# Decoder kernel on one core: router logits of the expert layer by feature in column strips, and a slot search with rounded 32-bit tables

## What is computed

```
full_logits = x @ gate_w.T                      # T = 4096 tokens, 8 dynamic experts and 1 fixed
# sparse mixer: 4 rounds of max / mask / softmax over the 8 dynamic logits -> sel, mult
rw = zeros(T, 8).at[rows, sel].add(mult)        # after a top-p cut, divided by its sum
mask_dyn = rw > 0
mask_dyn = mask_dyn * (cumsum(mask_dyn, axis=0) <= cap)    # cap = 640 tokens for each expert
gw = softmax(where(expert_mask == 0, -inf, full_logits))
out = sum_e global_w[:, e] * down_e(silu(x @ gate_e) * (x @ up_e))      # 8 dynamic, width 128
out += global_w[:, 8] * shared(x)                                       # fixed, width 512
```

## Time and profile before

| | |
|---|---|
| median of 3 runs | 2913.15 us (2906.86 to 2916.09) |
| the profiled execution's own time (span) | 2913.3 us |
| PE busy | 2502.7 us, 86% |
| DVE busy | 1650.9 us, 57% |
| ACT busy | 1352.2 us, 46% |
| POOL busy | 327.7 us, 11% |
| expert stage, first transpose to last shared_down | 1284.2 to 1615 us |

### The profile page before, as it was taken

One profiled execution on the slowest core, in us unless ns is written; L12 is line 12 of the kernel. 1 busy time (PEld: TensorE's weight loads), 2 busy tenths in 40 slices (PEclk: granted clock), 3 DMA queues, 4 the chain that ended last, 5 costly groups with the idle time before them and its releaser, 6 DMA issues. The chain is left out here.

```text
span 2913.3 us, 31557 instructions
## 1 busy us (share of the span) xinstructions
PE 2502.7 (86%) x11456; PEld 1482.0 (51%) x11456; DVE 1650.9 (57%) x3416; ACT 1352.2 (46%) x1966; POOL 327.7 (11%) x299
## 2 busy tenths in 40 slices
PE   6898898857888888879999699996688888887998
PEld 3665666533333333356456456655355555554565
DVE  6656666525566566715443698987656566632222
ACT  3333334313555555532122665663477777871211
POOL 1001101000000000000156300000211111100000
PEclk8989989967999899978799899998899999998999
DMA  2000000015333333240034511211200110002000
GB/s 75 15 15 14 16 8 18 12 52 121 53 66 68 61 65 59 44 160 3 18 60 64 98 66 37 73 44 45 99 8 30 37 37 22 22 8 65 22 15 22
DMA packets 104945, 132.41 MB, mean 45 GB/s; under 512 B 21748, under 2 KB 87556, under 8 KB 104792
## 3 DMA queue, kind: packets, MB, share of 16 engines
q1 hardware_dynamic: 90440, 115.58, 14.8%
q0 software_dynamic: 11904, 14.69, 3.1%
q10 hardware_dynamic: 2448, 0.14, 0.1%
HBM read 73.69 MB, written 31.20 MB: 36 GB/s over the span
## 5 line engine op out<-in xcount | busy, mean ns | idle before, releaser
L987 DVE TENSOR_REDUCE xattn_tops<-region 128x2 f32<-128x1024 f32 x256 | 306.2, 1219 | 127.1 <-PE region L771 127.0
L924 ACT ACTIVATE xattn_probs<-region 128x1024 f32<-128x1024 f32 x256 | 256.3, 1022 | 126.3 <-PE region L760 125.1
L2143 PE MATMUL region<-psi_fT 128*128 128x512 f32 x512 | 230.9, 597 | 10.3 <-ACT psi_fT L2267 7.1
L156 PE MATMUL region<-gla_xT,weights_even 128*128 128x512 f32 (+1 forms) x416 | 199.6, 634 | 20.2 <-ACT gla_xT L248 20.2
L760 PE MATMUL region<-xattn_qs,xattn_ks 49*128 49x512 f32 x512 | 125.9, 494 | 61.9 <-DVE xattn_tops L987 31.1
L2143 PEld LDWEIGHTS region<-psi_fT 128*128 128x128 f32 x512 | 93.6, 190 | 126.4 <-issue 115.0
L156 PE MATMUL region<-mamba_xT,weights_odd 128*128 128x512 f32 x320 | 154.2, 628 | 3.6 <-DVE mamba_xh L1966 3.6
L789 PE MATMUL region<-xattn_probs,xattn_va 128*32 128x512 f32 x1024 | 143.5, 628 | 1.2 <-ACT xattn_o_T L951 1.2
L156 PEld LDWEIGHTS region<-gla_xT,weights_even 128*128 128x128 f32 (+1 forms) x416 | 77.1, 192 | 132.2 <-issue 106.1
L771 PE MATMUL region<-xattn_ks,xattn_qs 48*128 48x512 f32 x512 | 125.8, 490 | 13.2 <-DMA xattn_ks<-xattn_khi 8.9
L165 PE MATMUL region<-weights_even,gla_work 128*128 128x256 f32 x512 | 119.3, 393 | 17.6 <-DVE gla_work L631 11.0
(11 more groups left out here) (500 smaller groups left out, 5134.8 us busy)
## 6 DMA issues: line engine op xcount, KB each, us to landing
weights_even<-mamba_cs SPq DMA_DIRECT2D x32, 512.0 KB, 4.7
xattn_qs<-xattn_qhi SPq DMA_DIRECT2D x128, 64.0 KB, 2.3
xattn_ks<-xattn_khi SPq DMA_DIRECT2D x128, 64.0 KB, 2.3
moe_sums<-moe_picked SPq DMA_DIRECT2D x9, 512.0 KB, 8.7
gla_x<-in_x SPq DMA_DIRECT2D x8, 512.0 KB, 3.8
x_after_gla<-gla_res SPq DMA_DIRECT2D x8, 512.0 KB, 2.9
xattn_x<-x_after_gla SPq DMA_DIRECT2D x8, 512.0 KB, 4.1
xattn_ctxT<-in_ctxT SPq DMA_DIRECT2D x8, 512.0 KB, 4.4
```

Of the source, the lines that this page charges most:

```text
L156: last = st.nc.tensor.matmul(o[0:m, i, :], w[:, c, col + i * P:col + i * P + m], rhs[:, c, :], start=c == 0, stop=c == kc - 1)
L924: A_(probs[:, p % 3, a, :, :], st.region(f"k{v}")[:], ACT.Exp).then_inc(st.emptying(f"k{v}"), 1)
L987: V.tensor_reduce(tops[:, n % 2, t, a::2], st.region(f"q{u}")[:], AX, ALU.max).then_inc(st.emptying(f"q{u}"), 1)
L2143: last = mm(o[:, a, :], fT[:, h, 0, t * P:t * P + P], fT[:, h, 1 + a, :], start=True, stop=True)
```

## The change

The logits are computed with `gate` (9 columns) as the stationary operand and 512 tokens moving, four elements to a group, each into its own 32 partitions (column strip) of one PSUM bank. ACT copies the bank into the buffer `silu`, four transposes (`by_token`) turn it back to tokens, and DVE copies from there. The two groups stand after `xT` 5 and between gate and up of u = 0; `by_token` stands ahead of gate in u = 0 and u = 1. Routing starts after u = 1 with two pieces there instead of with one after u = 0. In the slot search `table` and `holds` take the rounded type; the weights are split in a rounded high part and the rest, which is kept in the space of `mask` and gets a matmul of its own (128 columns) that adds to the first. `mask` takes the rounded type as well and is read as plain 32-bit by `count`.

```diff
@@ -1095,8 +1095,9 @@
         xe += [used[:, i * 1280:i * 1280 + 1280].rearrange("p (k d) -> p k d", k=SP_) for i in range(3)]
         rank8, reset = st.sb("rank8", [NE]), st.sb("reset", [NE, NX])
         run, cum = st.sb("run", [NE, NX]), st.sb("cum", [NE, NX])
-        weight, mask = st.sb("weight", [NX, NE + 1]), st.sb("mask", [NX, NE])
-        table, holds, ends = st.sb("table", [2, 3, P]), st.sb("holds", [2, CAP]), st.sb("ends", [2, 2])
+        weight, mask = st.sb("weight", [NX, NE + 1]), st.sb("mask", [NX, NE], F32R)
+        table, holds, ends = st.sb("table", [2, 3, P], F32R), st.sb("holds", [2, CAP], F32R), st.sb("ends", [2, 2])
+        weight_low = f3(mask[:].rearrange("p t e -> p (t e)"), 2)
         slot1, rank, spare = st.sb("slot1", [CAP]), st.sb("rank", [SP_]), st.sb("spare", [SP_])
         token_row, base_row = st.sb("token_row", [P]), st.sb("base_row", [P])
         ids, wslot = st.sb("ids", [NE, SP_]), st.sb("wslot", [NE, SP_])
@@ -1114,16 +1115,19 @@
         def order():
             for b in range(B):
                 yield "xT", b, 0
-                if b:
-                    yield "logits", b - 1, 0
-            yield "logits", B - 1, 0
+                if b == 5:
+                    yield "logits", 0, 0
             turned = {18: 0, 19: 1, 20: 2, 21: 3, 23: 4, 24: 5, 25: 6, 26: 7}
             for u in range(B * SHF):
                 b, f = divmod(u, SHF)
                 finds = [(u - 15, k) for k in range(SP_)] if 15 <= u < 15 + NE else []
                 if u in turned:
                     yield "turn_rows", turned[u], 0
+                if u < 2:
+                    yield "by_token", u, 0
                 yield "gate", b, f
+                if u == 0:
+                    yield "logits", 1, 0
                 for e, k in finds[0:2]:
                     yield "find", e, k
                 yield "up", b, f
@@ -1139,8 +1143,10 @@
                 for e, k in finds[4:]:
                     yield "find", e, k
                     yield "gather", e, 0
-                if u < 8:
+                if 1 <= u < 8:
                     yield "route", u, 0
+                    if u == 1:
+                        yield "route", 0, 0
                 yield from {7: [("exp", 0, 0)], 8: [("route", 8, 0)], 9: [("route", 9, 0)], 11: [("count", 0, 0)],
                             12: [("route", 10, 0)], 13: [("exp", 1, 0), ("route", 11, 0)],
                             14: [("turn", 0, 0), ("route", 12, 0)]}.get(u, [])
@@ -1168,7 +1174,6 @@
             @block.tensor
             def _(pe):
                 mm, tr = nc.tensor.matmul, nc.tensor.transpose
-                logits = flat(psum[REGIONS][:, 0:1, :])
                 for what, b, i in work:
                     if what == "xT":
                         pe.wait_ge(st.sem(f"x_in{b}"), 16)
@@ -1176,14 +1181,20 @@
                     elif what == "logits":
                         if b == 0:
                             weights.arrive(pe)
-                            logits = st.claim("logits", ring="bank")
-                        pe.wait_ge(*st.emptied(f"xT{b}"))
+                        o = st.claim(f"logits{b}", ring="bank")
+                        for a in range(4):
+                            pe.wait_ge(*st.emptied(f"xT{4 * b + a}"))
+                        for c in range(DC):
+                            for a in range(4):
+                                last = mm(o[32 * a:32 * a + NE + 1, :], gate[:, c, :], xT[:, 4 * b + a, c, :],
+                                          start=c == 0, stop=c == DC - 1)
+                        last.then_inc(st.filling(f"logits{b}"), 1)
+                    elif what == "by_token":
+                        pe.wait_ge(*st.emptied(f"logits{b}"))
+                        o = st.claim(f"by_token{b}", ring="bank")
                         for t in range(NT):
-                            for c in range(DC):
-                                last = mm(logits[:, 64 * b + 16 * t:64 * b + 16 * t + NE + 1],
-                                          xT[:, b, c, t * P:t * P + P], gate[:, c, :], start=c == 0, stop=c == DC - 1)
-                        if b == B - 1:
-                            last.then_inc(st.filling("logits"), 1)
+                            last = tr(o[:, t * P:t * P + P], silu[:, b, t * P:t * P + P], ident[:])
+                        last.then_inc(st.filling(f"by_token{b}"), 1)
                     elif what in ("gate", "up"):
                         o = st.claim(f"gu{b}_{i}") if what == "gate" else st.region(f"gu{b}_{i}")
                         a, w = (0, wg) if what == "gate" else (1, wu)
@@ -1204,8 +1215,8 @@
                         pe.wait_ge(st.sem("masked"), 1)
                         o = st.claim("count", ring="bank")
                         for a, w in enumerate((tri, ones)):
-                            last = mm(o[:, a * 256:a * 256 + 256], w[:], mask[:].rearrange("p t e -> p (t e)"),
-                                      start=True, stop=True)
+                            last = mm(o[:, a * 256:a * 256 + 256], w[:],
+                                      mask[:].rearrange("p t e -> p (t e)").bitcast(F32), start=True, stop=True)
                         last.then_inc(st.filling("count"), 1)
                     elif what == "turn":
                         pe.wait_ge(st.sem("weighed"), 1)
@@ -1233,7 +1244,9 @@
                         q = slice(32 * j, 32 * j + 32)
                         o = st.claim(f"find{b}_{i}", ring="bank")
                         mm(o[:, 0:3 * P], holds[q, g, i * P:i * P + P], table[q, g, :, :].rearrange("p a n -> p (a n)"),
-                           start=True, stop=True).then_inc(st.filling(f"find{b}_{i}"), 1)
+                           start=True, stop=False)
+                        mm(o[:, P:2 * P], holds[q, g, i * P:i * P + P], weight_low[q, g, :],
+                           start=False, stop=True).then_inc(st.filling(f"find{b}_{i}"), 1)
                     elif what == "turn_rows":
                         pe.wait_ge(st.sem(f"gathered{b % XE}"), 16 * SP_ * (b // XE + 1))
                         o = st.claim(f"xe{b}")
@@ -1296,9 +1309,14 @@
                     if what == "xT":
                         act.wait_ge(*st.full(f"xT{b}"))
                         A_(xT[:, b, :, :], st.region(f"xT{b}")[:], ACT.Copy).then_inc(st.emptying(f"xT{b}"), 1)
+                    elif what == "logits":
+                        act.wait_ge(*st.full(f"logits{b}"))
+                        A_(silu[:, b, :], st.region(f"logits{b}"), ACT.Copy).then_inc(st.emptying(f"logits{b}"), 1)
                     elif what == "up":
                         n = SHF * b + i
                         act.wait_ge(*st.full(f"gu{b}_{i}"))
+                        if n < 2:
+                            act.wait_ge(*st.full(f"by_token{n}"))
                         if n >= 2:
                             act.wait_ge(*st.emptied("gu{}_{}".format(*divmod(n - 2, SHF))))
                         A_(silu[:, n % 2, :], st.region(f"gu{b}_{i}")[:, 0, :], ACT.Silu).then_inc(st.sem("silu"), 1)
@@ -1423,7 +1441,7 @@
                     dve.wait_ge(*st.emptied("count"))
                     dve.wait_ge(st.sem("masked"), 1)
                     taken = r[:, TAKEN, :, 0:NE].rearrange("p t e -> p e t")
-                    step(STT(taken, run[:], CAP + 0.5, mask[:].rearrange("p t e -> p e t"), ALU.is_le, ALU.mult))
+                    step(STT(taken, run[:], CAP + 0.5, mask[:].rearrange("p t e -> p e t").bitcast(F32), ALU.is_le, ALU.mult))
                     TT(run[:], run[:], taken, ALU.mult)
                     step(TS(r[:, OPEN, :, :], r[:, TAKEN, :, :], 1e30, -1e30, ALU.mult, ALU.add))
                     step(TT(r[:, OUT, :, :], r[:, 0, :, :], r[:, TAKEN, :, :], ALU.mult))
@@ -1452,11 +1470,14 @@
                         last = TS(holds[:, g, :], slot1[:], ends[:, g, 1:2], None, ALU.is_gt)
                     step(last)
                     for g in range(2):
-                        last = STT(holds[:, g, :], slot1[:], ends[:, g, 0:1], holds[:, g, :], ALU.is_le, ALU.mult)
+                        last = STT(holds[:, g, :], slot1[:], ends[:, g, 0:1], holds[:, g, :].bitcast(F32), ALU.is_le,
+                                   ALU.mult)
                     step(last)
                     dve.wait_ge(*st.full("table"))
-                    V.tensor_copy(table[:, :, 0:2, :], st.region("table")[:, 0:4 * P].rearrange(
-                        "p (g a n) -> p g a n", g=2, a=2)).then_inc(st.emptying("table"), 1)
+                    o = st.region("table")[:, 0:4 * P].rearrange("p (g a n) -> p g a n", g=2, a=2)
+                    step(V.tensor_copy(table[:, :, 0:2, :], o))
+                    TT(weight_low, o[:, :, 1, :], table[:, :, 1, :].bitcast(F32), ALU.subtract).then_inc(
+                        st.emptying("table"), 1)
                     dve.wait_ge(*st.emptied("table"))
                     V.tensor_copy(m[:, 0, 0:1], m[:, 0, 0:1]).then_inc(st.sem("steps"), 1)
```

(11 more changed lines are left out.)

## The result

| | kernel before | changed kernel |
|---|---|---|
| median of the runs beside each other | 2914.62 us (2906.86 to 2925.87) | 2875.7 us (2862.98 to 2878.35) |
| ratio | | 0.9846 (0.9816 to 0.9876) |
| span of the profiled execution | 2913.3 us | 2876.3 us |

The forecast was 2872 us, range 2857 to 2889. The medians lie 38.9 us apart; the ratio's interval stands for 36 to 54 us, so the kernel is faster, by less than 2%.

The account below looks back on a forecast made before the run. The prediction took PE to pace the expert stage. Savings of 19.3 us (opening), 12.1 (u=15 to 17) and 9.6 (u=18 to 22) sum to 41.0, so 2913.3 us becomes 2872 us, range 2857 to 2889.

Parts of the forecast that it names:

- Opening: Stage's first transpose to end of unit 1's up: new logits order saves 19.3 us of PE time (17 to 24).
- I let the clock rise 5 us into the long matmuls, at 1308: In the opening: half clock until 1308, 23.8 us of work done by then, the other 13.7 taking 6.9.
- rival 2: Opening: clock rises during the transposes, at about 1290, since 9-column matmuls kept it down; 28 us saved, 2863; chance 0.08.
- The loads: Opening: row loads 1.5 us apart bring element 7 at about 1294.7, hidden by some 3 us, so no cost.
- Two pieces of routing after u = 1: DVE routes later, two pieces in one go; lag of about 4 us gone after u=5, cost 0.
- A find: Slot search: 0.37 us saved per find at full clock; 26 finds in u=18 to 22 give 9.6 us (5.2 to 11.2).
- u = 15 to 17: First slot searches and shared down: 12.1 us saved (6 to 19) from cheaper finds, less waits, plus a better clock.
- The clock: In u=15 to 17: clock back sooner, some 11 of the remaining 29 us at full, saving 5.5 us (0 to 13).
- Rival 1: Logits: column strips don't run side by side, 13.7 us per group at half; 13.3 us saved, 2878; chance 0.06.
- rival 3: Slot search: finds aren't cheaper, 40 x 0.2 to 0.4 us lost; 10 us saved in all, 2903; chance 0.05.
- Rival 5: u=18 to 22: cheaper finds leave PE gaps and the clock stays at 1.2 GHz; slower, 2939; chance 0.03.
- Rival 4: Scatter-adds: POOL takes over from add 1 on, some 6 us given back; 2878; chance 0.07.

Follow-up runs that it names:

- Experiment 4: Kernel before, with all eight elements transposed first and the 64 old 9-column logits matmuls after them; 2913.74 us, ratio 0.997.
- experiment 3: The changed kernel once more, without any edit; 2874.48 us beside 2917.77 of the kernel before, ratio 0.9839.
- experiment 2: Kernel before with only the slot search changed (rounded tables, second matmul per find), logits as before; 2905.66 us, ratio 0.9955.
- experiment 5: Changed kernel with the two loops of a logits group swapped, both feature halves of one strip before the next strip; 2879.27 us.
- experiment 8: Changed kernel with the first logits group after element 4 instead of 5; run twice, 2869.47 us and 2876.63 us (ratio 0.9847).
- experiment 6: Changed kernel with a throwaway copy of the first logits group, all in the first strip, ahead of the real one; 2869.24 us.
- experiment 9: Changed kernel with throwaway 512-column matmuls where PE waits, before the turn and before the first find; 2870.54 us, ratio 0.984.

## Why the prediction held, step by step

**The whole.** Forecast 41.0 us less; measured 38.9 and 43.3 by the medians of two comparisons, 45 and 47 by their ratios. The stage itself shrank by 46.8 and 53.7 us in the two profiles. That the median came within 4 us of 2872 is in part luck: one term was 8 us too small, and the medians happened to show less than the stage gained.

**Opening: right in mechanism, 8 us too small.** Forecast 19.3, measured 27.0. The terms held, taken at the full clock: a group 1.85 us (1.83 measured), the eight transposes back 1 us (two times 0.44). What failed is the step "I let the clock rise 5 us into the long matmuls, at 1308". It rose 5 us into the transposes. That is rival 2, to which I gave 0.08, with 28 us saved; it was nearly exact. Experiment 4 shows why before stayed at half for 40 us: not because of its transposes, as I had it in my sum, but because 9-column matmuls stood between them. By the Trainium skill, "TensorE: Matmul & The Clock Gate", Part 4, transposes don't count as busy for the clock; here they lifted it in experiment 4 and in all nine profiles with the new logits, 4.6 to 5.1 us behind the first transpose, so the measurement decides. I let that sentence keep me at the lower value.

**The loads: an error that the other one brought.** "Element 7 is there at 1294.7, hidden, by some 3 us" held for transposes of 1.76 us, though by the forecast's own times the margin was 1.3 us for element 5 and 5.6 for element 7. At the full clock the transposes of an element take 1.09 us, and the loads still come 1.5 us apart (1301.89 to 1303.39): PE waits 0.4 us for each of three, 1.3 us back. Without it, 28.3 would have been saved.

**Two pieces of routing after u = 1: right.** Unit 2 to turn took 69.3 us in both profiles. DVE's product for u = 6 still stands behind idle time, 4.3 us of the 7.1 in the earlier trace rows:

```profile
1342.83 0.69 DVE L1507 TENSOR_TENSOR moe_h<-moe_silu,region 128x512 f32<-128x512 f32 x1 [4.30 <-ACT moe_silu L1322]
```

**A find: right.** 0.37 us saved per find at the full clock forecast, (1.48 - 0.72) / 2 = 0.38 measured. From rows to the last find, with 25 finds, this gave 8.9 us; the 26th, the last of u = 17, stands ahead of the first transpose and gave 0.4 (0.84 us before, 0.43 after). So 9.3 instead of 9.6. Two of the three waits of 0.3 us for a bank before L1259 fall in here, which I hadn't looked for: with faster finds PE asks sooner for the bank that holds the output of `down`, which DVE (L1549) must read first.

**u = 15 to 17: right on the mean, for one part by chance.** Forecast 12.1, measured 11.4 in the first pair of profiles, 0.4 of it the find just named. The bank waits there, 0.76 and 0.91 us less the 0.52 of before, cost 1.2 against 1.4 priced. DVE's chain grew by 0.46 us, not 0.9. The comparisons that write the rounded type take 1.01 and 1.68 us for two as before, so they keep their speed; only the subtraction is new. The first row is from the profile before:

```profile
1406.76 1.01 DVE L1452 TENSOR_SCALAR moe_holds<-moe_slot,moe_ends 128x640 f32<-128x640 f32 x2
1390.85 1.01 DVE L1470 TENSOR_SCALAR moe_holds<-moe_slot,moe_ends 128x640 fp32r<-128x640 f32 x2
1394.33 0.42 DVE L1479 TENSOR_TENSOR moe_mask<-region,moe_table 128x256 fp32r<-128x256 f32 x1
```

The clock was the uncertain term. I had allowed 18 us at half between turn and rows (29 less 11); by the mean clocks it was 24 us in the first profile and 7 in experiment 3, against 37.6 before. With the old finds the stretch took 51.1 us three times and 41.7 once; with the new ones 39.7, 33.7, 36.2, 40.6, 41.9, 36.3 and 33.8 (experiments 3, 2, 5, 8, 8, 6 behind the first). The means differ by 48.8 - 37.5 = 11.3 us. Single profiles would give anything from 0 to 17. The changed kernel itself varies (39.7 and 33.7), but the 41.7 is the only profile with old finds and new logits, and the three of 51.1 all have the old logits: whether the new opening helps this stretch, or it was chance, one profile can't say.

Where the clock is better, PE waits more, which I had not priced. In experiment 3:

```profile
PE region L1246 <- DVE moe_picked L1524: 2.6, 2, 1.3
PE region L1211 <- DVE moe_h L1507: 1.4, 1, 1.4
```

That is 2.6 us for the banks of the finds instead of 1.7, and 1.4 us for DVE's product before `shared_down`, a wait that the first profile hasn't.

**The slower ones.** Rival 1 (serial strips) is refuted by experiment 6, rival 3 by the pair of 0.72 us. Rival 5: the clock is 1.00 from rows to the last find in every profile. Rival 4: POOL still waits 6.33 us for DVE before the sixth group, 8.25 in the earlier trace rows:

```profile
1535.36 1.55 POOL L1604 DMA_INDIRECT moe_sums<-moe_rt,moe_target  x1 [6.33 <-DVE moe_rt L1549]
```

**What stays open.** Why the earlier stages take 1276 to 1301 us with the same code: their share of half clock differs, but no run here takes that apart. And how far the clock's pattern in u = 15 to 17 could be steered: experiment 9 moved the fall by some us, and gained nothing.

## What to carry to other kernels

Where the stationary operand is the big one and only a few columns move, turn the matmul round and give several of them a column strip each: here 64 matmuls of 9 columns became 16 of 512, and the cost fell from 26.2 us (8 x 3.27) at the half clock to 3.7 plus a transpose back at the full one. Look at what stands between the dense work: here 9-column matmuls kept an engine that was never idle at half its clock, and the transposes between them paid too. When one engine's step gets twice as fast, ask again for each supply that was "hidden by 3 us": loads and banks were the next to be late.

## What the runs showed of the hardware that I had not expected

- Transposes of 128 columns in a row raised the clock from 0.50 to 1.00 in about 5 us (4.6 to 5.1 in ten profiles). 9-column matmuls back to back let it fall within 3 us and kept it at 0.50 for their other 22 us of unbroken work; it rose again 5.5 us into the 512-column matmuls behind them (experiment 4).
- Matmuls in free column strips start ahead of an earlier one whose strip is busy (1293.77 before 1294.19), and the order over the strips made no difference: 1.86 and 1.83 us (experiments 5 and 6).
- DVE wrote the rounded 32-bit type at the speed of the plain one: two comparisons of 640 elements took 1.01 us in both.
- A program whose profiles start the same stage over a range of 25 us needs a comparison by stages: the stage's own time separated 347 from 294 to 301 us, when the whole time left 0.98 to 0.99.
